# A macaron transformer block on one core: layer norms scaled on VectorE, k stored once, and a new table of step times

## What is computed

```python
x = x + 0.5 * _L0_ffn_ref(_layernorm(x), Wg, Wu, Wd)
x = x + _L0_attn_ref(_layernorm(x), w_q, w_k, w_v, w_o, rel_emb)
x = x + 0.5 * _L0_ffn_ref(_layernorm(x), Wg, Wu, Wd)

def _layernorm(x, axis=-1, eps=1e-05):
    m = jnp.mean(x, axis=axis, keepdims=True)
    v = jnp.var(x, axis=axis, keepdims=True)
    return (x - m) / jnp.sqrt(v + eps)
```

## Time and profile before

| | |
|---|---|
| median of 3 runs | 1380.19 us (1377.62 to 1382.7) |
| profiled execution | 1373.76 us, of it span 1371.8 us |
| busy: PE, DVE, ACT, POOL | 97%, 87%, 81%, 80% |
| mean granted TensorE clock | 0.989 of 2.4 GHz |
| DMA | 225 MB, nearly all in packets under 512 bytes |

### The profile page before, as it was taken

One profiled execution on the slowest core, in us unless ns is written; L12 is line 12 of the kernel. 1 busy time (PEld: TensorE's weight loads), 2 busy tenths in 40 slices (PEclk: granted clock), 3 DMA queues, 4 the chain that ended last, 5 costly groups with the idle time before them and its releaser, 6 DMA issues. The chain is left out here.

```text
span 1371.8 us, 29322 instructions
## 1 busy us (share of the span) xinstructions
PE 1333.0 (97%) x8472; PEld 1074.1 (78%) x8472; DVE 1192.4 (87%) x2554; ACT 1105.2 (81%) x2642; POOL 1098.6 (80%) x1012
## 2 busy tenths in 40 slices
PE   8999999999999999999999999999999899999798
PEld 7878777777878788778878878777888788788586
DVE  6887988998999999889899989899989889999465
ACT  6765878888888889878888888888888788888354
POOL 7977879788888888877779877889888788878465
PEclk9999999999999999999999999999999999999899
DMA  5404799999999999999999999999999989998200
GB/s 184 158 1 136 137 226 173 183 215 161 196 200 179 182 182 188 208 160 181 172 190 207 180 178 170 178 215 183 175 184 172 204 165 179 177 182 147 45 1 8
DMA packets 719138, 225.07 MB, mean 164 GB/s; under 512 B 653057, under 2 KB 698497, under 8 KB 718977
## 3 DMA queue, kind: packets, MB, share of 16 engines
q1 hardware_dynamic: 562224, 180.84, 73.4%
q10 hardware_dynamic: 156752, 42.36, 17.0%
HBM read 60.95 MB, written 69.86 MB: 95 GB/s over the span
## 5 line engine op out<-in xcount | busy, mean ns | idle before, releaser
L1231 POOL TENSOR_TENSOR hid_lo<-hid,hid_hi 128x512 fp32r<-128x512 f32 x512 | 662.1, 1302 | 149.2 <-ACT hid_hi L932 116.4
L1079 DVE TENSOR_TENSOR hid<-hid,work 128x512 f32<-128x512 f32 x512 | 347.1, 680 | 63.1 <-PE work L729 59.2
L1073 DVE SCALAR_TENSOR_TENSOR hid<-hid,work 128x512 f32<-128x512 f32 x512 | 345.2, 679 | 32.0 <-ACT hid L926 31.0
L1246 POOL TENSOR_TENSOR probs<-exps,probs 128x512 f16<-128x512 f32 (+1 forms) x288 | 307.2, 1069 | 79.0 <-ACT probs L989 76.0
L932 ACT CAST hid_hi<-hid 128x512 fp32r<-128x512 f32 x512 | 318.1, 625 | 62.0 <-DVE hid L1079 46.3
L926 ACT ACTIVATE hid<-work 128x512 f32<-128x512 f32 x512 | 307.1, 602 | 73.1 <-PE work L729 52.7
L977 ACT ACTIVATE exps<-work,negmax_shifted 128x512 f32<-128x512 f32 (+2 forms) x320 | 193.0, 605 | 40.9 <-DVE negmax_shifted L1179 25.4
L1173 DVE TENSOR_REDUCE negmax<-work 128x1 f32<-128x384 f32 (+3 forms) x352 | 222.2, 633 | 1.8
L727 PE MATMUL work<-xt,wg 128*128 128x512 f32 x512 | 205.3, 401 | 3.4 <-DVE xt L1048 1.5
L810 PE MATMUL acc<-hid_lo,wd 128*128 128x512 f32 x512 | 205.8, 405 | 0.8 <-POOL hid_lo L1231 0.7
L727 PE MATMUL work<-xt,wu 128*128 128x512 f32 x512 | 204.2, 399 | 1.0 <-DVE hid L1073 0.4
(11 more groups left out here) (99 smaller groups left out, 1909.2 us busy)
## 6 DMA issues: line engine op xcount, KB each, us to landing
prob_window_scratch<-probs SPq DMA_DIRECT2D x384, 80.0 KB, 3.0
rel_win<-rel_window_scratch ACTq DMA_DIRECT2D x250, 96.0 KB, 3.5
q_scratch<-rope SPq DMA_DIRECT2D x16, 512.0 KB, 4.7
qq<-q_scratch ACTq DMA_DIRECT2D x32, 256.0 KB
k_scratch<-rope SPq DMA_DIRECT2D x16, 512.0 KB, 3.9
rel_window_scratch<-g_s SPq DMA_DIRECT2D x32, 256.0 KB, 3.0
k_pad<-k_scratch SPq DMA_DIRECT2D x128, 64.0 KB, 3.1
prob_window_scratch<-probs SPq DMA_DIRECT2D x32, 256.0 KB, 4.8
```

Source lines behind the costliest of these rows:

```text
L1073: dve.scalar_tensor_tensor(out=hid[:, arg % HB, :], in0=hid[:, arg % HB, :], scalar=1.0, in1=work[bank_of["gate", arg]][:, :], op0=ALU.add ...
L1079: dve.tensor_tensor(hid[:, arg % HB, :], hid[:, arg % HB, :], work[bank_of["up", arg]][:, :], ALU.mult).then_inc(s_hid, 1)
L1231: pool.tensor_tensor(hid_lo[:, arg % HH, :], hid[:, arg % HB, :], hid_hi[:, arg % HH, :].bitcast(F32), ALU.subtract).then_inc(s_hlo, 1)
L1246: pool.tensor_tensor(probs[:, arg % PB, cols:2 * cols], exp_of(arg)[:, 0:cols], probs[:, arg % PB, 0:cols], ALU.subtract).then_inc(s_plent, 1)
```

## The change

- `ln_scaled` moves from ACT to DVE: four `tensor_scalar` of 128 columns, (x - mean) * rstd, the two scalars from `moments` and `rstd`. ACT's `Identity` activations go away, and with them POOL's steps for `mean_neg` and `shift`: POOL keeps `var_eps` and the power.
- k is written to scratch once instead of twice; `load_k` reads every row twice, by a step of 0, so it moves as many bytes as before. `v_add` waits for half as many increments.
- 14 idle transposes instead of 24.
- The first gate of a pass issues its two products on the upper part of x as soon as that is there, and waits for the rest of x only ahead of the third. (The planner wants `ln_hi` for it, `ln_lo` only in order.)
- `project_v` no longer waits in the plan for the store of k; all due times (`LATER`) are new, and `UNITS_TO` goes from 1406 to 1394.

```diff
-    UNITS_FROM, UNITS_TO = 146, 1406
+    UNITS_FROM, UNITS_TO = 146, 1394
...
-    LATER = {"acc": -121.4, "attention_sum": -318.4, "band_turn": -1036.1, "band_values": -446.9, "constants":
+    LATER = {"acc": -568.8, "attention_sum": -303.9, "band_turn": -586.9, "band_values": -750.7, "constants":
...
-        step("POOL", 1.85, time, "ln_rstd", what, ("ln_stats", what))
-        step("ACT", 1.55, time, "ln_scaled", what, ("ln_rstd", what))
+        step("POOL", 1.3, time, "ln_rstd", what, ("ln_stats", what))
+        step("DVE", 0.75, time, "ln_scaled", what, ("ln_rstd", what))
...
-                    base = t % VB * 4 * P * L
-                    for copy in range(2):
-                        sp.dma_start(bass.AP((q_t, k_t)[i], base + copy * (1 + i) * P * L,
-                                             [[L, P], [(2 - i) * P * L, 2], [1, L]]),
-                                     rope[:, :, :]).then_inc(s_qst[i], 16)
+                    if i == 0:
+                        for copy in range(2):
+                            sp.dma_start(bass.AP(q_t, (t % VB * 4 + copy) * P * L, [[L, P], [2 * P * L, 2], [1, L]]),
+                                         rope[:, :, :]).then_inc(s_qst[0], 16)
+                    else:
+                        sp.dma_start(bass.AP(k_t, t % VB * 2 * P * L, [[L, P], [P * L, 2], [1, L]]),
+                                     rope[:, :, :]).then_inc(s_qst[1], 16)
...
-            for i in range(24):
+            for i in range(14):
                 done = pe.transpose(work[0][:, 0:P], ident[:, :], ident[:, :])
...
-                        pe.wait_ge(s_xlo, LN["ln1" if kind == "A" else "ln3", t] + 1)
-                    bank = take_bank(name, arg)
-                    three(bank[:, :], wg[:, HI, e, cols], wg[:, LO, e, cols],
-                          x_hi, x_lo).then_inc(s_gate, 1)
+                    bank = take_bank(name, arg)
+                    pe.matmul(bank[:, :], wg[:, HI, e, cols], x_hi, start=True, stop=False)
+                    pe.matmul(bank[:, :], wg[:, LO, e, cols], x_hi, start=False, stop=False)
+                    if k == 0:
+                        pe.wait_ge(s_xlo, LN["ln1" if kind == "A" else "ln3", t] + 1)
+                    pe.matmul(bank[:, :], wg[:, HI, e, cols], x_lo, start=False, stop=True).then_inc(s_gate, 1)
...
-            def norm_scaled(m, x, sums):
-                act.wait_ge(s_shift, m + 1)
-                wait(act, s_xnt, m)
-                wait(act, s_ftok, sums)
-                for i in range(NT):
-                    done = act.activation(xn[:, i * P:(i + 1) * P], x[:, i * P:(i + 1) * P], ACT.Identity,
-                                          scale=rstd[:, i:i + 1], bias=shift[:, i:i + 1])
...
+            def norm_scaled(m, x, sums):
+                dve.wait_ge(s_rstd, m + 1)
+                wait(dve, s_xnt, m)
+                wait(dve, s_ftok, sums)
+                for i in range(NT):
+                    done = dve.tensor_scalar(xn[:, i * P:(i + 1) * P], x[:, i * P:(i + 1) * P], moments[:, i, 0:1],
+                                             rstd[:, i:i + 1], ALU.subtract, ALU.mult)
...
-                pool.tensor_tensor(mean_neg[:, :], zeros[:, :], moments[:, :, 0], ALU.subtract)
                 pool.wait_ge(s_ve, m + 1)
                 pool.tensor_tensor(rstd[:, :], var_eps[:, :], minus_half[:, :], ALU.pow).then_inc(s_rstd, 1)
-                pool.wait_ge(s_rstd, m + 1)
-                pool.tensor_tensor(shift[:, :], mean_neg[:, :], rstd[:, :], ALU.mult).then_inc(s_shift, 1)
```

More of the change, by code:

```diff
@@ L119, in step @@
-    def step(engine, takes, time, name, arg, *after, lands=None):
-        before = ()
+    LATER = {"acc": -568.8, "attention_sum": -303.9, "band_turn": -586.9, "band_values": -750.7, "constants":
+             921.7, "down": 32.9, "down_lo": -77.2, "exp": -141.1, "fill": 869.7, "gate": 23.3, "gated": -27.6, "hi": 25.4,
+             "largest": -268.3, "ln_hi": -210.8, "ln_lo": -619.1, "ln_rstd": 840.0, "ln_scaled": -20.6, "ln_stats":
+             -1358.2, "ln_turned": -51.0, "lo": -217.0, "load_band": -1016.9, "load_expert": -1131.9, "load_k": 374.4,
+             "load_q": -293.9, "load_window": 31.9, "load_x": -220.9, "near": -19.5, "outproj": 22.9, "p_hi": -212.1,
+             "p_lent": -548.5, "p_lo": -1294.9, "p_turn": 29.6, "prepare_hi": -155.0, "prepare_lo": 732.9, "product":
+             -80.6, "project": -185.5, "project_v": 45.4, "qk_hi": -423.8, "qk_lo": -1324.6, "qk_store": -277.2, "qrel":
+             30.1, "qrel_copy": -204.7, "qrel_store": -557.4, "recip": -955.6, "recip_copy": -41.3, "recip_turned": 48.5,
+             "recip_wide": -427.4, "rotate": 582.1, "scale": -456.1, "scores": -124.7, "shift": -383.4, "split_hi": -272.2,
+             "split_lo": -117.5, "store": 428.0, "store_band": -373.4, "sum": 34.3, "sum_turned": -698.3, "tanh": -225.1,
+             "up": 26.9, "v_add": 814.6, "v_split": -9.8, "values": -484.2, "zero": 1650.1}
@@ L121, in step @@
+    def step(engine, takes, time, name, arg, *after, lands=None, ordered=()):
+        before = []
         if name in ("p_lo", "p_lent", "shift"):
@@ L1130, in _ @@
                     norm_stats(LN[arg], x_s[t % XB])
+                if name == "ln_scaled":
+                    norm_scaled(LN[arg], x_s[arg[1] % XB], sums_before[arg])
                 if name == "ln_lo":
```

47 lines of the change are left out of this document (16 added, 31 removed).

## The result

The changed kernel takes 1543.2 us (median; 1542.8 to 1543.8), the kernel before 1378.9 on the same chip: a ratio of 1.119, with an interval of 1.116 to 1.122. The profiled execution has a span of 1541.3 us and a mean granted clock of 0.947 (before 1371.8 and 0.989). The forecast was 1380.5, with a range of 1366 to 1396.

A forecast was written before the change was run, and what follows sets the result against it. TensorE, busy 97%, was taken as the bound, DVE next at 87%. Junction -9.7, start -0.8, other first gates -0.7, k 0 and DVE's wait +11.5 gave +0.3 us: 1380.5 us, range 1366 to 1396.

The forecast's parts named there:

- k stored once: k's store and load, with POOL's and ACT's lighter work: counted as 0, with a gain or loss of 5 us.
- no wait of TensorE names that queue: SP's DMA queue: one 512 KB DMA less per sequence saves 0.6 us of issuing, eight times, without any TensorE wait there.
- ±5 us: All queues being re-dealt: a gain or loss of 5 us around a count of 0.
- DVE's wait for POOL: Each ln_scaled piece on DVE waits for POOL's running instruction: 2.9 us per norm, 11.5 us on the total, bounds 0 and 53.
- The rival without a shared port: DVE's scaling does not wait for POOL, and the start gains 3.3 us: 1366.5 us, chance 0.07.
- Taking off too the DVE idle time in the first 7 us behind each norm, in which it catches up: Step in pricing DVE's scaling: lowers the 25 us passed on to TensorE to 11.5.
- The junction from B6 to B7: Last norm overlaps B6's end: gap 4.2 us instead of 13.0, clock stays up through gaps under 1.5; -9.7 us.
- The start: First gate no longer waits for ln_lo: -0.8 us, at 10.6 instead of 11.40, bounds -3.3 and +2.
- DVE's share of the body: Stretch 150 to 1285 us: DVE's work grows by 55 us to 1085; a share of 95% or more would show it.
- DVE becomes the bound: DVE's queue behind ln_scaled in the body: 25 us without catching up, 1394 us, chance 0.2.

The follow-up runs named there:

- gate_and_14: The kernel before with only the first gate's split wait and 14 idle transposes instead of 24, scaling on ACT: 1373.5 us, ratio 0.998.
- order_kept: gate_and_14 with the norms' scaling on DVE, planner untouched, so the old order, k stored and read twice: 1406.8 us, ratio 1.022.
- k_twice_act: k_twice with the norms' scaling back on ACT and POOL's two small steps, same new order: 1404.8 us, ratio 1.022.
- k_twice: The changed kernel with k stored twice and loaded as before; new order and scaling on DVE stay: 1416.7 us, ratio 1.030.
- kept_and_half: order_kept with two more tensor_scalar of 112 columns on DVE ahead of each norm's four, into an unread tile: 1432.0 us, ratio 1.041.

## Why the prediction was wrong, point by point

The two-by-two of the order and the scaling, k stored twice, as ratios to the kernel before:

| | scaling on ACT | scaling on DVE |
|---|---|---|
| old order | 0.9976 (`gate_and_14`) | 1.0221 (`order_kept`) |
| new order | 1.0215 (`k_twice_act`) | 1.0299 (`k_twice`) |

From `k_twice` to the changed kernel it is 1.119. With 1376 us for a ratio of 1: -3 for the start and the gates, +34 for the scaling, +11 for the order, +123 for k's load, 164 us in sum before rounding. By the other way round the order has 33 and the scaling 12; the parts are not independent. The order's share is net of what it gains at the end of B6 (below).

- **k stored once: the step that failed.** "It moves as many bytes" was true (221 MB and 225), and "I count 0", within 5 us, was wrong by 123. The prediction counted bytes and issues, and asked whether TensorE waits for that queue. It did not read the access pattern of the load, whose first dimension is 2 in the changed kernel, so that its packets run two at a time. And its "no wait of TensorE names that queue" misreads the rows: the first of them, 10.9 us for `probs_t<-probs`, is for transposes that SP issues, from the queue of k's loads. In the old order that is the wait that grew, to 36.1 us; in the new one it was ACT that was held, through its own DMA queue.
- **The order: ±5 us was far too narrow.** It costs 33 us with the scaling on ACT, 11 with it on DVE. The text treated the redeal as a small error of both signs around a sum of parts. Four orders that differ from the old one in the planner's numbers alone, with every instruction the same, cost 11, 39, 39 and 93 us.
- **DVE's wait for POOL: mechanism right, price wrong.** The group of 96 in the changed kernel, and two norms on DVE's timeline, the first with POOL's rows beside it:

```profile
L1041 DVE TENSOR_SCALAR xn<-x,moments,rstd x96: 333/342/1447, 6.4 to 1466.4; 128x128 f32<-128x128 f32 x96
```
```profile
45.53 4.99 DVE L1041 TENSOR_SCALAR xn<-x,moments,rstd 128x128 f32<-128x128 f32 x4 [0.74 <-POOL rstd L1218]
...
616.66 1.11 DVE L1041 TENSOR_SCALAR xn<-x,moments,rstd 128x128 f32<-128x128 f32 x4
```
```profile
45.46 1.29 POOL L1211 TENSOR_TENSOR wg<-probs_t,wg 128x512 fp32r<-128x512 f32 x1
46.72 1.28 POOL L1211 TENSOR_TENSOR wu<-probs_t,wu 128x512 fp32r<-128x512 f32 x1
47.96 1.26 POOL L1211 TENSOR_TENSOR wg<-probs_t,wg 128x512 fp32r<-128x512 f32 x1
49.18 2.50 POOL L1229 TENSOR_TENSOR hid_lo<-hid,hid_hi 128x512 fp32r<-128x512 f32 x2
```

  At 616.66, with POOL idle (its next row comes at 617.88), four pieces take 1.11 us (the estimate was 0.87); at 45.53, beside an unbroken POOL, 4.99, which is as long as four of POOL's instructions. In all it is 58.7 us over 24 norms, 2.45 us each, where 2.9 had been forecast, and a mean of 672 ns, just under the 0.7 that the prediction named. The rival without a shared port is out, and the rule of the Trainium skill, "SBUF — State Buffer", section "Who interferes with whom", holds here. The price failed: 11.5 us were forecast from the old order's slack, and in that order it is 33. The failing step is "Taking off too the DVE idle time in the first 7 us behind each norm, in which it catches up". Without it the working gave 25, with every us passed on 53; in `kept_and_half` nothing of the added time is caught up, as 14.3 us more on DVE cost 25.2. That the new order has 11.9 is no confirmation of the working, which knew nothing of that order.
- **The junction from B6 to B7: about right, but for the clock.** TensorE in the changed kernel:

```profile
1463.61 0.50 PE L812 MATMUL acc<-hid_lo,wd 128*128 128x512 f32 x1 [0.34 <-POOL hid_lo L1229]
1464.89 0.63 PE L733 MATMUL work<-ident,xn 128*128 128x128 f32 x4 [0.78 <-ACT xn L934]
1466.92 0.63 PE L733 MATMUL work<-ident,xn 128*128 128x128 f32 x4 [1.40 <-DVE xn L1041]
1468.22 0.79 PE L788 MATMUL work<-xt,wg 128*128 128x512 f32 x1 [0.68 <-ACT xt L942]
1468.81 0.63 PE L789 MATMUL work<-xt,wg 128*128 128x512 f32 x1
...
1471.37 0.43 PE L728 MATMUL work<-xt,wu 128*128 128x512 f32 x1
```

  From the last down product to the first gate it is 4.6 us instead of 13.0; 4.2 was the forecast. The wait for the last `hid_lo` came to 0.34 us. But behind gaps of 0.78, 1.40 and 0.68 us the clock is at the lower level, which the prediction had thought such gaps would not do: the eighth matmul starts 3.15 us behind the first, 0.45 us from one to the next instead of 0.227, so 1.6 us are still lost. The twelfth matmul of B7 starts 8.7 us behind the last down product (1472.34), before 17.7 (1303.32). Less the 1.1 us for the band product and `outproj`, the gain is 7.9 us instead of 9.7.
- **The start: a loss, not a gain.** The first gate comes at 11.10, not at 11.40 or the forecast 10.6. The scaling took what the prediction feared, beside POOL's split of the weights:

```profile
6.37 3.18 DVE L1041 TENSOR_SCALAR xn<-x,moments,rstd 128x128 f32<-128x128 f32 x4 [1.49 <-POOL rstd L1218]
```
```profile
9.70 0.63 PE L733 MATMUL work<-ident,xn 128*128 128x128 f32 x4 [2.64 <-DVE xn L1041]
11.10 0.77 PE L788 MATMUL work<-xt,wg 128*128 128x512 f32 x1 [0.77 <-ACT xt L911]
```

  The 14 transposes end early and TensorE idles for 2.64 us. Behind that the first six matmuls run at the lower clock, and the twelfth starts at 15.02 us, where it was 14.01 before: 1.0 us lost, 0.2 of it by a later landing of the identity matrix, for the 0.8 forecast as gained; that is inside the bounds of -3.3 and +2.
- **DVE's share of the body, "95% or more".** The prediction's 1085 of 1135 us are 96%, not the 97% that it names. The stretch of the changed kernel has 83%, since everything there is slower; `k_twice` has 92%. The two rows, in this order (busy us of PE, PEld, DVE, ACT, POOL):

```profile
150.00:1285.00 1135.00, 1015.02 (x6488) 802.98 (x6487) 938.75 (x2052) 816.46 (x2003) 807.40 (x721) 0.94 0.98 157
```
```profile
150.00:1285.00 1135.00, 1088.07 (x7253) 867.04 (x7252) 1043.38 (x2275) 911.88 (x2242) 897.39 (x799) 0.98 0.98 179
```

  The rival "DVE becomes the bound" named the right place and had the right sign, with 25 us for what costs 33 in the old order. None of the rivals had k's load in it.

**What stays open.** Why an order is 30 us slower was not found. The two causes that were tried, the places of k's and q's loads, were not it. Whether a wider first dimension for q's load, whose packets run four at a time before and after the change, would gain something was not tried.

## What to carry to other kernels

Read the first dimension of both sides of every DMA that a change rewrites, not its bytes: a repeat written as an outermost dimension of 2 cost 7% in one order and 9% in the other. Then ask who else uses the queue and the DMA engines: in one order the transposes of the same queue paid for it, in the other the engine that issued on another queue. In a schedule that was found by search, no edit is local: price a redeal by building the edit in the old order and in the new, and give it a range of several per cent, not of the size of its parts. And don't take idle time of a neighbour off a price unless a trace shows it being used.

## What was not expected of the hardware

- A DMA issue can hold an engine for long: ACT's issue of one window load took up to 9.86 us (0.62 in the median), 28 of 253 over 1.5 us; before, the longest was 2.76 and 5 were over 1.5.
- Ten idle transposes fewer brought nothing at the start of `gate_and_14`: TensorE idles for 1.39 us ahead of the first norm's transposes, and the first gate, which comes 1.5 us sooner, has lost that lead by the eighteenth matmul, since about nine before it run at the lower clock (0.63 us each instead of 0.39).
- Four `tensor_scalar` of 128 columns with two scalars take 1.11 us while POOL is idle, and 4.99 beside an unbroken POOL.
